# The expert stage of a decoder kernel: hidden values made transposed, gates repeated by DMA

## The reference

```python
def _L1_ffn_ref(x, W1, b1, W2, b2, Wr, br):      # x is the layer-normed input
    K = 2                                        # 16 experts of 64 hidden values, width 128
    xf = x.reshape(-1, D)
    logits = xf @ Wr + br
    _, topk_idx = jax.lax.top_k(logits, K)
    mask = jnp.zeros_like(logits).at[jnp.arange(T)[:, None], topk_idx].set(1.0)
    gates = mask + logits - jax.lax.stop_gradient(logits)
    h = jax.nn.relu(jnp.einsum('td,edh->eth', xf, W1) + b1[:, None, :])
    combined = jnp.einsum('te,eth,ehd->td', gates, h, W2) + gates @ b2
    return x + combined.reshape(B, S, D)
x = x + _L1_ffn_ref(_layernorm(x, axis=-1), ...)
```

## Time and profile before

| | |
|---|---|
| median of 3 runs | 4045.31 us (4044.43 to 4045.65) |
| profiled execution, its own time | 4050.56 us |
| its span | 4048.8 us |
| mean granted clock of TensorE | 0.983 |
| busy in the span | PE 3845.5 us (95%), DVE 2922.8 (72%), ACT 2792.6 (69%), POOL 1902.7 (47%) |
| the expert stage, from its first statistics | 3689.8 us to the end, about 359 us |
| SP's last four loads of the first stage, issued in this order | cross weights 1536 KB, state weights 2438.5 KB (11.9 us to landing), steps 350 KB, cross bias repeated to 128 rows, 64 KB |
| first and last addition of y to x | 3705.62 and 4045.69 us |

### The profile page before, as it was taken

How to read it: one execution, slowest core, us unless ns; L and a number is a source line. 1 busy time by engine, 2 the same in 40 slices (tenths; PEclk the granted TensorE clock), 3 DMA queues, 4 the chain that set the end, 5 groups by cost and what they waited for, 6 DMA issues and landing times. The chain is left out here.

```text
span 4048.8 us, 109312 instructions
## 1 busy us (share of the span) xinstructions
PE 3845.5 (95%) x35786; PEld 3012.5 (74%) x35786; DVE 2922.8 (72%) x7397; ACT 2792.6 (69%) x6292; POOL 1902.7 (47%) x1726
## 2 busy tenths in 40 slices
PE   8999899999989999898999989999999989998999
PEld 6777687888756666675666677888888867776777
DVE  7888655555479999658999955776777767775665
ACT  5555455555579999747999965777777767774333
POOL 5555322222278888526777753333333321112444
PEclk9999899999989999999999999999999989999999
DMA  1000100000100000100000010000000000000000
GB/s 30 19 19 19 52 7 6 6 6 6 41 9 8 8 8 8 29 16 9 8 8 8 12 29 30 1 0 0 0 0 0 0 3 3 3 3 6 12 12 13
DMA packets 118477, 46.71 MB, mean 12 GB/s; under 512 B 92256, under 2 KB 117088, under 8 KB 117728
## 3 DMA queue, kind: packets, MB, share of 16 engines
q1 hardware_dynamic: 118368, 45.30, 4.3%
HBM read 24.36 MB, written 4.19 MB: 7 GB/s over the span
## 5 line engine op out<-in xcount | busy, mean ns | idle before, releaser
L1102 POOL TENSOR_TENSOR l_rc<-l_rc,l_rs 128x1024 f32<-128x1024 f32 x128 | 303.7, 2373 | 202.3 <-DVE l_rs L1294 193.0
L1169 ACT ACTIVATE l_prob<-l_prob,l_mx 128x128 f32<-128x128 f32 x1024 | 312.9, 393 | 0.0
L670 POOL TENSOR_TENSOR ca_prob<-ca_prob,ca_sm 128x1232 f32<-128x1232 f32 x64 | 144.0, 2250 | 299.3 <-DVE ca_sm L836 299.3
L1780 POOL TENSOR_TENSOR mb_steps<-w_upto,mb_dta 128x1024 f32<-128x1024 f32 x64 | 121.5, 1898 | 345.7 <-DVE mb_dta L2048 345.7
L1194 PE MATMUL l_qk_ps<-w_local,l_hT 128*128 128x512 f32 x512 | 249.1, 610 | 13.0 <-DVE l_rs L1294 11.2
L1096 POOL TENSOR_TENSOR l_prob<-l_prob,l_sm 128x1024 f32<-128x1024 f32 x128 | 243.0, 1898 | 20.5 <-DVE l_sm L1280 20.5
L1079 POOL TENSOR_TENSOR l_rc<-l_rc,l_ss 128x1024 f32<-128x1024 f32 x128 | 243.6, 1903 | 12.5 <-POOL l_rc L1102 4.5
L1939 PE MATMUL mb_x_ps<-w_wx,mb_xT 128*128 128x256 f32 x1024 | 237.2, 385 | 0.0
L382 ACT ACTIVATE la_ef<-la_feat,la_fbias 128x1024 f32<-128x1024 f32 x128 | 135.7, 1111 | 121.8 <-PE la_feat L441 121.8
L2507 POOL TENSOR_TENSOR mo_hid<-mo_hid,mo_gate 128x1024 f32<-128x1024 f32 x64 | 121.8, 1903 | 201.3 <-DVE mo_hid L2653 201.3
L346 POOL TENSOR_SCALAR la_ef<-la_ef,la_high,la_low 128x1024 f32<-128x1024 f32 x128 | 151.4, 1193 | 134.6 <-ACT la_ef L382 134.6
(11 more groups left out here) (349 smaller groups left out, 11860.7 us busy)
## 6 DMA issues: line engine op xcount, KB each, us to landing
la_xin<-in_x SPq DMA_DIRECT2D x64, 64.0 KB
la_xT<-in_x_T SPq DMA_DIRECT2D x64, 64.0 KB, 1.8
l_h<-lt_y SPq DMA_DIRECT2D x128, 32.0 KB
lt_quad<-lt_y SPq DMA_DIRECT2D x32, 128.0 KB
out_x<-k_x SPq DMA_DIRECT2D x64, 64.0 KB, 1.5
l_h<-lt_y SPq DMA_DIRECT2D x128, 31.8 KB
lt_quad<-lt_y SPq DMA_DIRECT2D x32, 127.0 KB
ca_ctxT<-in_ctx_T SPq DMA_DIRECT2D x128, 19.2 KB
```

The costliest lines, as they stand in the source:

```text
L1102: gp.tensor_tensor(wide(rc[l][:]), wide(rc[l][:]), wide(rs[l][:]), ALU.add).then_inc(*pool_sum.did("rot"))
L1169: ex = sc.activation(p[:, a, j], p[:, a, j], ACT.Exp, bias=mx[l][:, a, j:j + 1])
```

## The change

The hidden values are computed already transposed (hidden index on the partitions, tokens along the row): w1 is the stationary side, xnT the moving one, in eight blocks of 128. ACT adds b1 as a column bias and applies the Relu while it evacuates each block. The gates then have to be multiplied in along the tokens and repeated over the 64 rows of each expert: PE transposes them (from a buffer by_half of 128 columns, the 16 gates ordered by half, the rest zero), ACT copies them to SBUF, SP writes the 16 rows to a small DRAM buffer (parked), waits until they have landed, and loads each half of them into 64 partitions. DVE multiplies them into hidT. The product of gates and b2 uses all 128 rows. The pipeline gets the parts STAT, TURN, ROUTE, GATE, WAIT, SPREAD and OUT with lags 0 to 6, seven in place of five, and four steps to a trip of the loop; hidT and gateT have four buffers, hid_ps two in the place of turn_ps. POOL keeps the addition of xn alone.

```diff
-    "experts": (("w1", 1024), ("w2", 1024), ("b2", 128), ("wr", 16), ("b1", 1024), ("br", 16)),
+    "experts": (("w1", 1024), ("w2", 1024), ("b2", 128), ("wr", 16), ("b1", 8), ("br", 16)),
...
+        hidT = [m.sb(f"hidT{i}", [128, CH, T]) for i in range(4)]
+        gateT = [m.sb(f"gateT{i}", [128, T]) for i in range(4)]
+        spread = both(m, "spread", [128, CH, T])
+        hid_ps = m.ps("hid_ps", [128, 2, CH, T])
...
+        STAT, TURN, ROUTE, GATE, WAIT, SPREAD, OUT = range(7)
...
             @block.sync
-                    b = at(LAST)
+                    b = at(GATE)
+                    if b:
+                        sp.wait_ge(*act_gate.at("gT", b))
+                        sp.dma_start(g.parked[b.lane], gateT[b.slot][0:E]).then_inc(parked[b.lane], 16)
+                        sp.wait_ge(parked[b.lane], b.loaded())
+                        for a in (0, 1):
+                            src = g.parked[b.lane].rearrange("(a j) t -> a (j t)", a=2)[a].partition_broadcast(64)
+                            sp.dma_start(spread[b.lane][64 * a:64 * a + 64].rearrange("p j t -> p (j t)"), src).then_inc(spread_in[b.lane], 16)
+                    b = at(OUT)
...
             @block.gpsimd
-                        gp.tensor_tensor(hid[l][:], hid[l][:], gate[l][:].unsqueeze(2).to_broadcast([T, E, HID]), ALU.mult
-                                         ).then_inc(*pool_hid.did("hid"))
-                    b = at(NORM)
+                    b = at(TURN)
                     if b:
                         gp.wait_ge(*vec_norm.at("xn", b))
                         gp.tensor_tensor(one(b), one(b), xn[b.lane][:], ALU.add).then_inc(*pool_norm.did("xr"))
...
             @block.scalar
+                    b = at(GATE)
+                    if b:
+                        sc.wait_ge(*pe_gate.at("gT", b))
+                        sc.wait_ge(*pe_out.at("y", b, ago=4))
+                        sc.wait_ge(*vec_hid.at("hid", b, ago=2))
+                        sc.activation(gateT[b.slot][:], gate_ps[:, 0:T], ACT.Copy).then_inc(*act_gate.did("gT"))
+                    b = at(STAT)
...
+                    b = at(TURN)
+                    if b:
+                        sc.wait_ge(*pe_turn.at("xnT", b))
+                        sc.wait_ge(*pe_route.at("h1", b, ago=2))
+                        sc.activation(xnT[b.lane][:], xn_ps[:, 0:T], ACT.Copy).then_inc(*act_turn.did("xnT"))
+                    b = at(ROUTE)
+                    if b:
                         for u in (0, 1):
+                            sc.wait_ge(*pe_route.at(f"h{u}", b))
+                            sc.wait_ge(*pe_out.at("y", b, ago=4))
+                            for j in range(4 * u, 4 * u + 4):
+                                ex = sc.activation(hidT[b.slot][:, j], hid_ps[:, b.lane, j], ACT.Relu, bias=b1[:, j:j + 1])
+                            ex.then_inc(*act_hid.did(f"h{u}"))
...
             @block.tensor
+                    b = at(GATE)
+                    if b:
                         te.wait_ge(*vec_route.at("gate", b))
+                        te.wait_ge(*act_gate.at("gT", b, ago=1))
+                        te.transpose(gate_ps[:, 0:T], by_half[b.lane][:], g.ident[:]).then_inc(*pe_gate.did("gT"))
                     b = at(TURN)
                     if b:
                         te.wait_ge(*vec_norm.at("xn", b))
                         te.wait_ge(*act_turn.at("xnT", b, ago=1))
                         te.transpose(xn_ps[:, 0:T], xn[b.lane][:], g.ident[:]).then_inc(*pe_turn.did("xnT"))
+                    b = at(OUT)
+                    if b:
+                        te.wait_ge(*vec_hid.at("hid", b))
+                        te.wait_ge(*vec_out.at("x", b, ago=1))
+                        for j in range(CH):
+                            te.matmul(y_ps[:, 0:C], hidT[b.slot][:, j], w2[:, j], start=(j == 0), stop=False)
+                        te.matmul(y_ps[:, 0:C], gateT[b.slot][:], b2, start=False, stop=True).then_inc(*pe_out.did("y"))
                     b = at(ROUTE)
                     if b:
                         l = b.lane
                         te.wait_ge(*act_turn.at("xnT", b))
                         te.wait_ge(*vec_route.at("logit", b, ago=1))
                         te.matmul(route_ps[:, 0:E], xnT[l][:], wr, start=True, stop=True).then_inc(*pe_route.did("r"))
+                        te.wait_ge(*act_hid.at("h1", b, ago=2))
                         for u in (0, 1):
                             for j in range(4 * u, 4 * u + 4):
+                                mm = te.matmul(hid_ps[:, l, j], w1[:, j], xnT[l][:], start=True, stop=True)
+                            mm.then_inc(*pe_route.did(f"h{u}"))
...
             @block.vector
+                    b = at(TURN)
+                    if b:
+                        l = b.lane
+                        v.wait_ge(*act_norm.at("rstd", b))
+                        v.wait_ge(*pe_turn.at("xnT", b, ago=2))
+                        v.wait_ge(*pool_norm.at("xr", b, ago=2))
+                        v.tensor_scalar(xn[l][:], one(b), mv[l][:, 0:1], rstd[l][:, 1:2], ALU.subtract, ALU.mult
+                                        ).then_inc(*vec_norm.did("xn"))
+                    b = at(SPREAD)
+                    if b:
+                        hid = hidT[b.slot][:]
+                        v.wait_ge(*act_hid.at("h1", b))
+                        v.wait_ge(spread_in[b.lane], b.loaded(32))
+                        v.tensor_tensor(hid, hid, spread[b.lane][:], ALU.mult).then_inc(*vec_hid.did("hid"))
+                    b = at(STAT)
...
-                    b = at(LAST)
+                    b = at(OUT)
...
-                        v.tensor_copy(chosen[l][:, 0:K], top[l][:, 0:K]).then_inc(*vec_route.did("chosen"))
+                        v.memset(top[l][:, K:8], LOW).then_inc(*vec_route.did("chosen"))
...
-                pipeline(v, g.NB, LAST + 1, step)
+                pipeline(v, g.NB, OUT + 1, step, turn=4)
```

More of the change, by code:

```diff
@@ L2441, in experts @@
         part = g.experts_part
-        w1 = part["w1"].rearrange("p (e h) -> p e h", e=E)
+        w1 = part["w1"].rearrange("p (j n) -> p j n", j=CH)
         w2 = part["w2"].rearrange("p (j c) -> p j c", j=CH)
-        b2, wr, b1, br = part["b2"][0:E], part["wr"], part["b1"], part["br"]
+        b2, wr, b1, br = part["b2"], part["wr"], part["b1"], part["br"]
         eps = m.sb("eps", [128, 1])
@@ L2488, in step @@
                         sp.dma_start(dst, src).then_inc(g.stored, 16)
-                pipeline(sp, g.NB, LAST + 1, step)
+                pipeline(sp, g.NB, OUT + 1, step, turn=4)
                 sp.wait_ge(g.stored, 16 * g.NB)
@@ L2497, in _ @@
                     gp.memset(logit[l][:], LOW).then_inc(zeroed, 1)
[L2498 removed]
+                    gp.memset(by_half[l][:], 0.0).then_inc(zeroed, 1)
                 pool_norm.start(gp)
[L2500 removed]
                 def step(at):
[L2503 to L2506, removed]
[L2507 to L2509 removed]
+                    b = at(TURN)
                     if b:
@@ L2512, in step @@
                         gp.tensor_tensor(one(b), one(b), xn[b.lane][:], ALU.add).then_inc(*pool_norm.did("xr"))
-                pipeline(gp, g.NB, LAST + 1, step)
+                pipeline(gp, g.NB, OUT + 1, step, turn=4)
             @block.scalar
@@ L2543, in step @@
                         sc.wait_ge(*pe_turn.at("xnT", b))
+                        sc.wait_ge(*pe_route.at("h1", b, ago=2))
                         sc.activation(xnT[b.lane][:], xn_ps[:, 0:T], ACT.Copy).then_inc(*act_turn.did("xnT"))
-                pipeline(sc, g.NB, LAST + 1, step)
+                    b = at(ROUTE)
+                    if b:
+                        for u in (0, 1):
+                            sc.wait_ge(*pe_route.at(f"h{u}", b))
[3 more added lines that the diff above has]
+                            ex.then_inc(*act_hid.did(f"h{u}"))
+                pipeline(sc, g.NB, OUT + 1, step, turn=4)
             @block.tensor
             def _(te):
-                for stage in (pe_turn, pe_route, pe_out):
+                for stage in (pe_turn, pe_route, pe_gate, pe_out):
                     stage.start(te)
@@ L2570, in step @@
                         te.matmul(route_ps[:, 0:E], xnT[l][:], wr, start=True, stop=True).then_inc(*pe_route.did("r"))
[L2571 to L2579 removed]
+                        te.wait_ge(*act_hid.at("h1", b, ago=2))
                         for u in (0, 1):
                             for j in range(4 * u, 4 * u + 4):
[L2582 to L2594 removed]
+                                mm = te.matmul(hid_ps[:, l, j], w1[:, j], xnT[l][:], start=True, stop=True)
+                            mm.then_inc(*pe_route.did(f"h{u}"))
+                pipeline(te, g.NB, OUT + 1, step, turn=4)
             @block.vector
             def _(v):
[L2598 removed]
+                for stage in (vec_stat, vec_norm, vec_hid, vec_route, vec_out):
                     stage.start(v)
@@ L2665, in decoder @@
```

(1 more changed line is left out.)

102 lines of the change are left out of this document (25 added, 77 removed).

## The result

| | us | |
|---|---|---|
| kernel before, median of 5 runs | 4044.95 | 4043.26 to 4045.65 |
| changed kernel, median of 5 runs | 4025.02 | 4022.40 to 4025.89 |
| ratio | 0.9950 | 95% interval 0.9939 to 0.9962 |
| changed kernel, profiled execution | 4023.55 | span 4021.4 |

What follows compares the result with a forecast made beforehand. The prediction took a loop of latencies, 4.70 us a step, as the bound after the change: span 3708 + 290 + 5.4 = 4003.4, 45.4 below 4048.8, so a median of 4000 us, range 3978 to 4040.

Steps and rivals of the forecast that it cites:

- The loop of latencies: Last stage's cycle xn, its transpose, y and routing on PE, DVE's addition and routing chain, next xn: forecast bound, 4.70 us.
- about 6 us less: Drain: without routing, y of batch 63 comes about 6 us earlier than 63 x 4.70 = 296, so 290.
- Sum 4.70 us, ends 4.6 and 4.8: Steady step of the last stage: PE 2.11, wait to y's addition 0.475, routing chain 1.63, xn 0.34, wait 0.15.
- D = 5.6, and the ring has 2.2 us to spare: Gate copy to landed reads: parking 1.8, two wakes 0.1 each, loads 3.6; two spread buffers allow 7.85 us.
- L: Short for the loop of latencies through y's addition, routing chain, xn and its transpose; forecast at 4.70 us a step.
- I cost the clock at nothing: PE's clock in the last stage: stays at 1.00 despite idling about 0.5 of 4.7 us, so no time was added.
- rival 2: DMA ring or ACT's Relus stretch the last stage's step to 4.85 to 5.35 us, around 4028; chance 0.22.
- Rival 1: PE stays the bound as loop waits are overestimated: step 4.25 to 4.45 us, time 3978; chance 0.10.
- The prediction's sign of being wrong: DVE idle before its product, ended by a DMA, would mean the ring through the DMAs decides, not the loop.
- Rival 3: Slower: repeated reads of one 4 KB piece are slow, deciding above 7.3 us; 4063 to 4200 us; chance 0.14.
- Rival 4: PE not shortened: 128-column products with new weights take 0.14 us a pass, 38 passes 5.3; 4038; chance 0.04.
- 38 passes in 4.22: PE's work per step after the change: gate 1, xn 1, y 16, b2 2, routing 2, hidden 16; 4.22 us.

Runs made afterwards that it cites:

- e1: Changed kernel with four spread buffers in place of two, the gate copy waiting for the product of four batches earlier: 4021.4 us, ratio 0.9940.
- e12: e9 with xn still made early but the gate transpose back at the head of TensorE's step: 4021.6 us, ratio 0.9940.
- e4: Changed kernel with three quarters of the repeated gates left out of the reads, every instruction kept: 4012.3 us, ratio 0.9921.
- e5: e4 with eight steps to a trip of the hardware loop in place of four: 4001.3 us, ratio 0.9892.
- e2: Changed kernel with the output store issued by GpSimd instead of SyncE: 4022.1 us, ratio 0.9943.
- e3: Changed kernel with the parking write issued by ScalarE on its own queue instead of by SyncE: 4018.8 us, ratio 0.9935.
- e7: Changed kernel with each repeated read filling every second partition instead of 64 neighbouring ones, weights permuted to suit: 4015.2 us, ratio 0.9928.
- e8: Changed kernel, full reads, xn made a step earlier and the gate transpose moved to the middle of y: 4023.2 us, ratio 0.9945.
- e6: e4 with xn made a step earlier and the gate transpose moved to the middle of y: 3974.3 us, ratio 0.9827.
- e9: Changed kernel with the edits of e7 and e8 together, nothing left out: 3985.1 us, ratio 0.9849.

## Why the prediction was wrong

The loop of latencies as the bound and the sign were right, the size was not. The span was forecast at 3708 + 290 + 5.4 = 4003.4 and is 4021.4, 18 us more; the median was forecast at 4000 and is 4025.0, 25 more. The 7 us between the two lie outside the pieces below: the traced execution of the kernel before was 5.6 us over its median (4050.56, 4044.95) and that of the changed kernel 1.5 under its own. Where in the program they arise, one trace of each does not tell. Piece by piece:

- **Start of the first y**: 3705.4 instead of 3708. The stage itself began 2.1 us earlier than in the trace of before (first statistics 3687.61, not 3689.75), with nothing of the changed stage ahead of it but the load of its weights; in the traces of e1 to e12 this start lies anywhere from 3684.20 to 3687.97. Less this, the fill is +3.9, forecast +4.5. Right.
- **From the first y to the last**: 310.6 instead of 290 (3705.35 to 4015.99). This is the whole miss. Of it 1.8 is the first y at clock 0.51, 3.62 us for 16 passes instead of the 1.8 to 2.0 of others: TensorE had stood idle 2.96 us just ahead, for gates that VectorE makes behind its first product, and that product had waited 2.33 us for its reads. 13 are in the 58 steps that follow, 4.92 instead of 4.70 each, and 6 in the last five, 23.2 instead of the 17.5 that 4.70 and "about 6 us less" make.
- **After the last y starts**: 5.4, as forecast.

**"Sum 4.70 us, ends 4.6 and 4.8"** is the step that failed. Its terms were read from steps of the kernel before, where TensorE is busy throughout and nothing shows of what the turn of the hardware loop costs. In a closed loop of latencies nothing hides it: the sum lacked a term of 1.35 us a trip, 0.34 a step (e4 against e5). The rest of the sum was 0.14 too large (4.56). Together +0.20 a step, 11 of the 13 us. The rows of the kernel before did not give it away: a trip has two steps there, and the weight loads of the gate transpose are 5.43 apart whether a turn lies between or not (3835.61, 3841.04, 3846.47). I priced no engine's own turn.

**"D = 5.6, and the ring has 2.2 us to spare"** failed too, by its length and its form. The parking takes 2.9 us instead of 1.8, the reads 4.5 (alone) instead of 3.6: D is about 7.6. It still fits into 7.85, and e1 shows that opening this ring alone gains nothing. But the transfers close another loop over *one* step, which the text did not form: the parking of a step has to get past the reads of the step before, and the next reads wait for it, 4.8 to 5.0 us round. It costs 0.04 a step, 2 us in all, only because L is 4.90 anyway (e2, e3, e4, e7); opening L shows what the transfers allow (e8). "Behind them on SP waits only the output store" overlooked that SyncE's own next parking stands behind its reads.

**"About 6 us less"** for the drain was right without the transfers (e4's last five steps take 16.4) and lost with them: there the product waits 2.3 to 3.7 us in each step, and the transfers are the bound. In the timeline of the changed kernel's drain:

```profile
4004.45 1.23 DVE L2617 TENSOR_TENSOR mo_hidT<-mo_hidT,mo_spread 128x1024 f32<-128x1024 f32 x1 [2.33 <-DMA mo_spread<-parked]
...
4009.25 1.22 DVE L2617 TENSOR_TENSOR mo_hidT<-mo_hidT,mo_spread 128x1024 f32<-128x1024 f32 x1 [3.38 <-DMA mo_spread<-parked]
...
4010.82 3.31 PE L2580 MATMUL mo_y_ps<-wl_experts,mo_hidT 128*128 128x128 f32 x16 [2.56 <-DVE k_x L2629]
...
4014.42 1.22 DVE L2617 TENSOR_TENSOR mo_hidT<-mo_hidT,mo_spread 128x1024 f32<-128x1024 f32 x1 [3.74 <-DMA mo_spread<-parked]
```

The pitch is 4.8 and 5.2 us. The 16 passes of 4010.82 take 3.31 us, those of the step before 2.02: after 2.56 us of waiting TensorE was mostly at the lower of its two clocks, 1.2 GHz (granted clock 0.57 in these 3.31 us; behind a wait of 1.50 it was 1.00). "I cost the clock at nothing" held in the steady part (1.00 throughout), not at the two ends.

**The rivals.** The time fell near the 4028 of rival 2 and the step inside its 4.85 to 5.35, but neither of its causes is at work: not the ring of buffers (e1), not the Relus. Rival 1 is refuted by TensorE's idle time, and e6 shows what it would have taken. The prediction's sign of being wrong, idle time of VectorE before the product that a DMA ends, did appear (34.7 us, 47 times), and it misled: with that wait gone the step was still 4.90 (e2, e3, e7). Such a row tells that two loops are near each other, not which one binds. Rival 3: a repeated read is not slow, 4.5 us for the pair against the 7.3 from which it decides. Rival 4: a pass takes 0.11 us.

**Right, by the rows**: 38 passes in 4.22 (e6: 4.26). The product 1.23 us, as the earlier trace rows had it. ScalarE no bound: eight Relus in 2.17 us, under the estimate of 2.5. DMA engines busy about half of their time (0.47). GpSimd's work down to its addition of xn. No mo_turn_ps.

**The port shared by VectorE and GpSimd.** In the changed kernel the product is usually late, so GpSimd's addition is done before it: 0.455 us in the mean. Where the product follows xn directly, the two collide. (In e7, where GpSimd issues no store, the mean is 1.26 too.) The group of that line in the changed kernel, then in e2:

```profile
L2516 POOL TENSOR_TENSOR k_x<-k_x,mo_xn 128x128 f32 x51 | 23.2, 455 | 228.1 <-DVE mo_xn L2610 228.1
```

```profile
L2509 POOL TENSOR_TENSOR k_x<-k_x,mo_xn 128x128 f32 x51 | 63.3, 1242 | 43.6 <-DVE mo_xn L2610 43.6
```

1.24 us instead of 0.46, and the product stays at 1.22: the narrow addition is held until the wide product ends (3854.11 to 3855.35 in e2, the product 3853.82 to 3855.04), and nobody waits for it, as the sum had it. That agrees with the Trainium skill, "SBUF — State Buffer", section "Who interferes with whom", by which the two engines take a shared port in turn.

**The reads to the two halves.** Alone the pair takes 4.53 us to the start of the product, between the 3.6 of the sum and the 5.4 that serialized halves would give; with the destinations interleaved 4.18, and engines busy for 0.38 instead of 0.47 at equal traffic. The Trainium skill, "SBUF — State Buffer", section "Can I just issue two DMAs to hit both halves?", says that transfers to the two halves serialize instead of adding up. The direction agrees, the full serialization is not seen. That the layout of the destination matters is shown by e7, and by e9 against e8, 38 us; whether the port or something else in the path does it, no run tells.

## What to carry to other kernels

When an engine that was busy all the time gets less work, write down every cycle that now closes around it, over one step as well as over the number of buffers, with each in-order queue as a member, and price in each the turn of the hardware loop, which a saturated engine hid. If two cycles come out within a few per cent, expect little from opening either alone and test them together: here the fixes gave 2 us (e8, not to be told from nothing) and 10 (e7) singly and 40 together (e9). Price the fill and the drain by themselves: here transfers had no cover there, and TensorE, having waited for them, ran passes at the lower clock.

## What the runs showed of the hardware

- The turn of a hardware loop costs 1.35 us a trip where a chain of short waits between engines is the bound (e4, e5), against 0.15 where TensorE is busy throughout (e6: the step of the turn 4.37, the others 4.22 in the mean).
- A parking of 8 KB takes 1.4 us with idle engines. Issued 1.9 us behind 512 KB of repeated reads it takes 3.0 in the mean, from another engine's queue too (e3: 3.1); issued 3.5 behind, 1.34 (e2).
- Two repeated reads of 256 KB each: 4.53 to 4.79 us to the first product with each in 64 neighbouring partitions, 3.91 to 4.18 with every second one; a parking 1.9 us behind them 3.1 (e8) and 2.4 (e9) in the mean.
- The first y passes at clock 0.51 take 3.62 us for 16, those at 1.00 between 1.8 and 2.0.
